# One exponential operation for two score steps in a fused attention block

## The reference

```python
xn = group_norm(x) * gn_w + gn_b                    # 32 groups
qkv = einsum('oc,bct->bot', qkv_w, xn) + qkv_b      # 8 heads of 64 channels
weight = softmax((q * scale)^T @ (k * scale), over keys)
a = einsum('bts,bcs->bct', weight, v)
out = xn + einsum('oc,bct->bot', proj_w, a) + proj_b
```

## Time and profile before

| | |
|---|---|
| time, median of 3 runs | 3720.25 us (3719.15 to 3724.84) |
| profiled execution: time, span | 3719.26 us, 3717.6 us |
| TensorE clock granted, mean | 0.999 of full |
| busy share of the span | PE 99%, PEld 61%, DVE 57%, ACT 77%, POOL 82% |
| chain that ended last | PE 97%, ACT 1%, DVE 1% |

### The profile page before, as it was taken

One profiled execution on the slowest core, in us unless ns is written; L12 is line 12 of the kernel. 1 busy time (PEld: TensorE's weight loads), 2 busy tenths in 40 slices (PEclk: granted clock), 3 DMA queues, 4 the chain that ended last, 5 costly groups with the idle time before them and its releaser, 6 DMA issues.

```text
span 3717.6 us, 74814 instructions
## 1 busy us (share of the span) xinstructions
PE 3691.2 (99%) x30104; PEld 2271.1 (61%) x30104; DVE 2101.8 (57%) x2798; ACT 2877.4 (77%) x4091; POOL 3050.6 (82%) x1718
## 2 busy tenths in 40 slices
PE   8999999999999999999999999999999999999999
PEld 5565565656756565565675656556577565656657
DVE  6555556555555555655555555565555555555564
ACT  3777777888677777788767777788876777777886
POOL 1888888898389888888938898888874888989893
PEclk9999999999999999999999999999999999999999
DMA  2000012011400001211130000111123000000022
GB/s 82 21 17 26 23 33 74 21 57 34 152 20 22 18 24 32 74 35 43 51 134 25 18 23 17 56 51 46 41 77 103 23 20 23 21 20 20 19 83 96
DMA packets 132282, 165.03 MB, mean 44 GB/s; under 512 B 61792, under 2 KB 107872, under 8 KB 131424
## 3 DMA queue, kind: packets, MB, share of 16 engines
q1 hardware_dynamic: 131936, 160.26, 13.8%
HBM read 122.17 MB, written 38.04 MB: 43 GB/s over the span
## 4 chain that ended last, share of the span: by engine, by line
PE 97%; ACT 1%; DVE 1%; issue 0%; POOL 0%; DMA 0%; SPq 0%; ACTq 0%; POOLq 0%; DVEq 0%
PE oacc L661 31%; PE scores L637 24%; PE pool_bank L579 14%; PE aux_banks L601 13%; PE pool_bank L591 7%; PE scores L738 5%; PE pool_bank L624 2%; ACT probs L847 1%; PE scores L579 1%; ACT scores L860 0%; DVE stats L995 0%; DVE maxima L967 0%; POOL denom L1240 0%; PE scores L591 0%; DMA xn<-x 0%
## 5 line engine op out<-in xcount | busy, mean ns | idle before, releaser
L1240 POOL TENSOR_TENSOR denom<-denom,probs 128x768 f32<-128x768 f32 x1528 | 2797.5, 1831 | 373.4 <-ACT probs L847 192.0
L967 DVE TENSOR_REDUCE maxima<-aux_banks 128x2 f32<-128x512 f32 x1728 | 1657.5, 959 | 1450.6 <-PE aux_banks L601 1416.8
L847 ACT ACTIVATE probs<-scores 128x768 f32<-128x768 f32 x1728 | 1308.8, 809 | 656.5 <-PE scores L637 600.6
L860 ACT ACTIVATE scores<-seeds 128x768 f32<-128x768 f32 x1728 | 1339.5, 819 | 2.2 <-PE scores L645 1.5
L661 PE MATMUL oacc<-probs,vals 128*64 128x384 f32 x6912 | 1282.6, 492 | 0.0
L661 PEld LDWEIGHTS oacc<-probs,vals 128*64 128x64 f32 x6912 | 455.2, 136 | 519.7 <-issue 371.1
L601 PE MATMUL aux_banks<-k_hi,q_hi 64*128 64x512 f32 (+1 forms) x3456 | 680.9, 390 | 4.9 <-DVE maxima L967 4.9
L601 PEld LDWEIGHTS aux_banks<-k_hi,q_hi 64*128 64x128 f32 x3456 | 321.9, 183 | 531.4 <-issue 441.8
L637 PE MATMUL scores<-q_hi,k_hi 64*128 64x384 f32 x3456 | 591.6, 338 | 7.1 <-ACT scores L860 7.1
L637 PE MATMUL scores<-q_hi,k_lo 64*128 64x384 f32 x3456 | 587.0, 335 | 0.0
L637 PE MATMUL scores<-q_lo,k_hi 64*128 64x384 f32 x3456 | 586.7, 334 | 0.0
(11 more groups left out here) (96 smaller groups left out, 1558.3 us busy)
## 6 DMA issues: line engine op xcount, KB each, us to landing
seeds<-neg_rows SPq DMA_DIRECT2D x96, 384.0 KB, 3.5
xtile<-x SPq DMA_DIRECT2D x72, 384.0 KB, 3.2
att<-o_norm SPq DMA_DIRECT2D x96, 192.0 KB, 2.4
probs<-x SPq DMA_DIRECT2D x18, 768.0 KB, 4.6
out<-probs SPq DMA_DIRECT2D x18, 768.0 KB, 3.7
xtile<-att SPq DMA_DIRECT2D x12, 768.0 KB, 4.6
att_raw<-att SPq DMA_DIRECT2D x12, 768.0 KB, 6.3
neg_rows<-neg_cols SPq DMA_DIRECT2D x384, 0.8 KB
```

The source lines that it names most:

```text
L847: a(prob(s).rearrange("p (h n) -> p h n", n=N), scores[:, s % 2, :, 0:N], ACT.Exp, scale=SCALE).then_inc(probs_ready, 1)
L860: a(scores[:, s % 2, :, 0:N], seeds[blk % 2][:, :].rearrange("p (e n) -> p e n", n=N), ACT.Copy).then_inc(seeded, 1)
L967: v.tensor_reduce(maxima[:, :, qt, kc], aux_banks[:, :, 0:UNIT_KEYS[kc % 2]], AX.X, ALU.max)\
L1240: gp.tensor_tensor(acc, acc, prob(s), ALU.add).then_inc(added, 1)
```

## The change

One ScalarE operation of 128x1536 takes the exponentials of both steps of a group, from all four banks of `scores` into two neighbouring places of the ring. It waits for the scores of the second step of the group, asks for the ring's room of both steps at once, and raises `probs_ready` by 2. Seeds, matmuls, the additions of GpSimd and all orders stay as they are.

```diff
                 if s >= RING:
-                    gone = s - RING
+                    gone = s + GS - 1 - RING
                     act.wait_ge(pv_done, PRIMED + BSTEPS * b + gone + 1)
                     act.wait_ge(added, PRIMED + ADDS * (BLOCKS * b + gone // KT) + max(1, gone % KT))
-                act.wait_ge(scores_full, BSTEPS * b + s + 1)
-                a(prob(s).rearrange("p (h n) -> p h n", n=N), scores[:, s % 2, :, 0:N], ACT.Exp,
-                  scale=SCALE).then_inc(probs_ready, 1)
+                act.wait_ge(scores_full, BSTEPS * b + s + GS)
+                first = s % RING * 2 * N
+                a(probs[:, first:first + GS * 2 * N].rearrange("p (s h n) -> p s h n", h=2, n=N),
+                  scores[:, :, :, 0:N], ACT.Exp, scale=SCALE).then_inc(probs_ready, GS)
...
                 for i in range(PAIRS * SLOTS):
-                    for s in range(GS * i, GS * i + GS):
-                        exponentials(s, b)
+                    exponentials(GS * i, b)
                     for s in range(GS * i + 2, min(GS * i + 4, BSTEPS)):
                         seed(s, b)
```

## The result

The changed kernel takes 3886.55 us (median of 4 runs, 3885.38 to 3890.51) against 3719.95 us, a ratio of 1.0445 (95% interval 1.0433 to 1.0458): slower by 4.5%, 167 us. I had forecast 3,926 us, 206 us more, in a range of 3,850 to 4,005.

A forecast was written before the change was run, and what follows sets the result against it. TensorE bounds; a 4.08 us loop lengthens shorter groups: 176.3 us (464 one-part or finish groups), 24.6 and 7.0 (nothing extra), -3.5 stall, +2 starts: 206 us more, 3,926 us. Range 3,850 to 4,005; the sum's own 3,895 to 3,955.

The forecast's parts named there:

- What bounds the kernel: TensorE, busy 99%; seeds ready ahead of its arrival by 0.45 us (last used) and 0.66 us (first).
- Item 1: Loop's first term: the pair exponential of 1536 elements takes 1.46 us, bounds 1.40 and 1.62.
- Items 4 to 6: Second seed to its first matmul 0.06 us, to the step's last matmuls 0.45, to the next exponential 0.45.
- Item 2: From the pair operation's end to the first seed: 0.11 us, bounds 0.02 and 0.12.
- The two-part groups: Groups with two extra parts of TensorE work stay at 4.34 us, 0.26 us over the loop: no loss.
- The ring: Asking for both steps' room at once costs nothing; GpSimd lags less. Rival: 187 us on top, 4,113 us, chance 0.02.
- The stall that goes: In the last batch ScalarE's 3.46 us wait for GpSimd disappears: -3.5 us.
- The loop is shorter: Rival, chance 0.12: pair operation 1.40 us, gap to seed 0.02, loop 3.93 us, so 3,850 us.
- The pair operation saves nothing: Rival, chance 0.11: pair operation 1.62 us, loop 4.24 us, so 4,006 us.
- The late seeds are covered: Rival, chance 0.04: TensorE's other products hide the later seeds; not slower, 3,720 to 3,725 us, or 3,716.
- The clock falls: Rival, chance 0.04: TensorE's idles drop its clock to 1.2 GHz in 38 groups, 88 us more, 4,014 us.
- The rule: Skill's halves: grouping helps a saturated engine (43 us at most saved); otherwise smaller pieces finish sooner, so time rises.

The follow-up runs named there:

- late_start: Kernel before the change, still two exponentials per group, but both wait for the scores of the second step: 3844.60 us, ratio 1.0334.
- late_release: Kernel before the change, each exponential starting with its own scores, but only the second raises the count, by 2: 3727.94 us, ratio 1.0022.
- more_waits: Changed kernel with two more waits, both long met, ahead of each seed's own wait: 3930.41 us, ratio 1.0563.
- filler_768: Changed kernel with an unused 128x768 SBUF copy on ScalarE between the wide exponential and the seeds: 4274.58 us, ratio 1.1487.
- ring_pairs: Kernel before the change, one exponential per step, but the ring's room is asked for in pairs: 3720.07 us, ratio 0.9997.
- covered: Changed kernel with the wide exponential only in the 362 groups with two extra parts, one exponential per step elsewhere: 3728.66 us, ratio 1.0021.

## Why the prediction was right in kind and a quarter too large

**What bounds the kernel.** Right: TensorE's arrival against the seeds. The size of the margin I read too large. I counted 0.45 us up to the first matmul of the second step, but a wait has a price of its own: from the seeds' end to the last matmuls of the step it takes 0.05 + 0.46 = 0.51 us where TensorE waits (585.29 to 585.80, after), and in the kernel before it was 563.07 to 563.89, 0.82:

```profile
563.54 0.34 PE L637 MATMUL scores<-q_hi,k_hi 64*128 64x384 f32 x2
...
563.89 0.34 PE L637 MATMUL scores<-q_lo,k_hi 64*128 64x384 f32 x2
```

That leaves 0.31. late_start agrees: a start 0.52 us later lengthens the group by 0.22, so 0.30 were to spare. late_release takes 0.14 of it without lengthening the group. The forecast doesn't rest on the 0.45, since its sum goes around the loop and never uses the margin.

**The items of the loop.** Item 1, the wide operation: 1.46 predicted, 1.45 measured (1451 ns on average, 864 times, below), so the line through two copies holds for four banks. Item 3: 1.55 and 1.55. Items 4 to 6: 0.06 + 0.45 + 0.45 predicted, 0.05 + 0.46 + 0.46 measured (585.29, 585.34, 585.80, 586.26). Item 2 is the step that failed in size: from the operation's end to the first seed 0.11 predicted, 0.03 measured. These 0.08 us, in some 500 groups, are 40 us, all of the difference between 3,926 and 3,887. I took the 0.11 from the dependent pair behind a projection and did not look at what else that seed waits for: `seed(0)` there waits for three semaphores, `seed(s)` in the stream for one. more_waits shows that the waits make it: with three, gap and loop are the predicted ones. Nor is the 0.03 a matter of the wide operation: in late_release the seeds start 0.03 us (0.032, the median of 768) after an exponential of 128x768. My lower bound, 0.02, was nearly exact.

```profile
L848 ACT ACTIVATE probs<-scores 128x1536 f32<-128x1536 f32 x864 | 1253.8, 1451 | 749.0 <-PE scores L637 748.6
```

**The two-part groups.** Right: 4.35 before and after, until filler_768 takes the loop over them.

**The ring.** Right: 0.9997 for ring_pairs. GpSimd lags less than before (its waits for ScalarE at L1240 rise from 192 to 370 us), and ScalarE's waits for it are gone in the changed kernel.

**The stall that goes.** Right in sign: no wait of ScalarE for GpSimd is left in the profile after, so the 3.46 us are gone.

**The rivals.** *The loop is shorter* came as near as my own sum, 3,850 against the measured 3,887 and my 3,926, by one of its two parts: its gap of 0.02 nearly holds (0.03), its wide operation of 1.40 does not (1.45). *The pair operation saves nothing* falls (1.45). *The late seeds are covered* falls in the groups of one part and is what happens in those of two; covered shows it, but for its 8 us. *The clock falls* does not happen: TensorE is granted 1.00 in the stretch of the shortest work (the granted clock is the column ahead of the DMA share):

```profile
3740.00:3820.00 80.00, 68.69 (x468) 34.07 (x466) 36.39 (x41) 64.95 (x71) 60.52 (x34) 1.00 0.30 107
```

TensorE is busy 86% of it, less than in the stretch of the earlier trace rows, at the same clock. The Trainium skill's case of a clock that swings with short idles (TensorE: Matmul & The Clock Gate, section on psum-queue depth-cycling) is not seen here.

**The rule.** Of the Trainium skill's two halves (Perfetto Trace Analysis, section Optimizing Scalar/DVE Operations) the second holds in this trace: ScalarE was not saturated, and its work in small pieces let TensorE go on sooner. ScalarE's busy time even rose, 2877 to 2921 us, since for the exponentials and seeds of a group it is busy 3.00 us now (1.45 and 1.55) against 2.95 (1.40 and 1.55): the overlap with the seed that is lost, 0.11, is more than the 0.06 that the wide operation saves (1.51 against 1.45).

**Where the profile differs from what I wrote.** I wrote that TensorE's busy share would fall to about 95%, and that its waits for L860 would rise to some 100 us or more. The share stays at 99%, because matmul rows overlap across the wait, and the waits are 29.3 us on PE and 174.8 on PEld; the time is to be read from the idle of the weight loads and from the distance of the groups.

## What to carry to other kernels

Before two operations are joined, draw the loop that they stand in, from the start of one to the start of the next, and compare it with the work that the bounding engine has in that time: joining makes the first half wait for the second's input (0.52 us here) and its users for the second's end (0.14), and what it saves on the engine was small beside them (0.06). Sum over the kinds of groups, since those with more work than the loop pay nothing, unless the joined engine has other work behind it in them (covered). When the price of a dependence comes from another place in the trace, count the waits that stand there too.

## What the runs showed that I had not expected

A wait that is already met is not free on ScalarE when it stands ahead of an instruction that waits for the one before it: with one wait the seed started 0.03 us after the exponential's end, with two 0.09, with three 0.11 (more_waits), and the two extra ones cost some 43 us in the kernel. A fourth added nothing: in more_waits the seeds that open a block have four, and the gap is 0.113 us as with three. And the time of the wide exponential, 1451 ns for 1536 elements from four banks against 809 for 768 from two, shows no price for the two further banks: 809 and 768 more elements at 0.847 ns would be 1459. (The four banks are evenly spaced, so whether a further dimension that can't be merged would cost something, this doesn't show.)
